# A state-space layer and experts: one scaled piece per unit moves from VectorE to GpSimd, and some buffers shift by six words

## The chip, the cores and the metric

The kernel runs on one NeuronCore of a Trainium2 chip. The metric is the device time of one execution in microseconds (us), lower is better. All arithmetic is float32. Five engines with queues of their own take part: TensorE (PE; its weight loads are shown as PEld), VectorE (DVE), ScalarE (ACT), GpSimd (POOL) and SyncE (SP, which only issues DMAs). They meet at semaphores.

## The reference, cut to what matters

2048 tokens are embedded (C = 192), normalised, and go through a selective state-space layer in both directions, then through eight experts of which each token takes two. What the change touches is the scan:

```python
xz = layernorm(x) @ W_in                       # 192 -> 2 * 384
u  = silu(depthwise_conv1d(xi, conv_w, conv_b))
for each direction d in (forward, backward):
    dt = softplus(u @ Wx[:, :12] @ dt_w + dt_b)          # per token and channel
    B, C = the next 16 and the last 16 columns of u @ Wx # per token and state
    h  = exp(dt * A) * h + (dt * u) * B                  # along the tokens, 16 states per channel
    y  = sum over states of h * C,  + u * D
y  = layernorm(merge of both) * silu(z);  out = y @ W_out + residual
then: layernorm, router (top 2 of 8), h = relu(x @ W1[e] + b1)**2, y = h @ W2[e] + b2
```

## The kernel before, in words

The tokens stand in NG = 4 groups of 512 (GT), a group in TG = 4 tiles of 128, the 384 channels in DB = 3 blocks of 128. A **unit** u is a pair of states in one direction of one group: UG = 16 units a group, NU = 64 in all; `unit_of(u)` gives group, pair and direction. An **item** i = 3u + blk is one block of channels of a unit, a tile of 128 x 1024 (two states by 512 tokens); there are 192.

The stage of the scan (about 184 to 668 us of the span) is a pipeline over four engines, each with its loop written out by hand:

- ACT, for each unit: `exps(u)`, six activations, two per block (L1206), that make the decay exp(dt * A); then `scale_x(u + 1)`, seven activations (L1192), that scale seven of the eight pieces (two states by four tiles, each 128 x 384) of the transposed dt * u by a column of B. A piece lands in `xt(u % 2, n, t)`. `exps(u)` waits for the scans of unit u - 2 (decay is double by direction), `scale_x(u + 1)` for the transposes of unit u - 1 (`s_x_ps`).
- DVE, for each item: `scan(i)` (L818) with the decay from SBUF and the input from PSUM; it waits for the decay, for the transposed input (`s_x_ps`) and for the sum of item i - 4 (`s_sum`; there are four state buffers). Among the scans stand: `scale_rest(u + 2)` (L837), the eighth piece, after the third scan of each unit; `keep_dtu_t` (L844), a copy from PSUM in eight of the 16 units of the first three groups; and, at the start of a group, `keep_y` (L823) and `moments_y` (L635, L638) of the group before.
- POOL, for each item: state = state * C in place (L559), C coming broadcast by DMA (L456) in `c_bc[u % 3]`. In units 4 and 9 of the first three groups it also makes dt * u for the next group, `times_u` (L548).
- PE, for each item: `x_transposes_of(i)`, eight transposes of scaled pieces into a pair of PSUM banks (waits for scan i - 2, and for a new unit for `s_xt_a` and `s_xt_v`); then `add(i - 3)`, eight transposes that add the states into the y banks (waits for `s_mul`). All transposes stand at L1376.

PE's wait for the input of a new unit:

```python
if blk == 0:
    pe.wait_ge(s_xt_a, u + 1)
    pe.wait_ge(s_xt_v, u + 1)
```

After the last item everything waits for `s_sum` = 192: ACT and SP then issue the loads of gates and expert weights (L1236, L477), and the out product, router and experts follow.

Before the stage, DVE and POOL work on softplus: DVE `correction` (L772, L773) and `dt_sum` (L779), POOL L543, and DVE `times_u` for group 0 (L787). In the front part POOL makes the gate terms (L538).

**Where the buffers lie.** They are cut one after another from one SBUF tensor, `arena`, in words of four bytes. All sizes up to `xt_flat` are multiples of 16 words, so `u_all`, `dt_all`, `bt`, `c_bc[1]`, `c_bc[2]`, `decay` and `state` start on a grid of 16 words. Each of the two `xt_flat` has three words more (`DB * (ODD - P)`: the eighth piece has its blocks 129 words apart), so what is cut after them, `dtu_t[1]`, `dtu` and `c_bc[0]`, starts six words off that grid. Hence of the three C buffers, the one of the units with u % 3 = 0 is six words off already before the change, the other two are on the grid. `state`, which is multiplied with them, is on the grid.

Of the kernel before, what the change touches and what calls it, by code (L numbers as in the profile page):

```python
# [8 lines left out]
ALU = mybir.AluOpType  # L9
# [12 lines left out]
DB = DI // P  # L22
NS = 16
RANK = 12
GT = 512
NG = TOK // GT
TG = GT // P
SG = GT // SEQ
PAIR = 2
UG = 2 * (NS // PAIR)  # L30
NU = NG * UG
# [16 lines left out]
BATCHES = (0, 2, 8, 16, 24, 32, SLOTS)  # L48
HH = H // 2
GATE_W = 2 * TG * DI  # L50


class Steps:
# [17 lines left out]
def build(nc, tok, emb, spos, pos, chan, w_in, gb_in, xproj, dt_w, gb_out, w_out, merge, w_route, emb_t,  # L71
          energy, fatigue, gates12, b1, b2, wf1, ws1, hf1, wf2, ws2, hf2, gates_dram, b_rows, x_rows, y_rows, out):
    ctx = ExitStack()
    with ctx:
# [3 lines left out]
        def sem(name):  # L78
            return ctx.enter_context(nc.semaphore(name))
# [57 lines left out]
        used = [0]  # L137

        def cut(shape, dt=FP32, parts=P):
            n = 1  # L140
            for s in shape:
                n *= s
            words = n if dt != BF16 else n // 2
            assert used[0] + words <= ARENA, used[0]
            v = arena[0:parts, used[0]:used[0] + words]
            used[0] += words
            if dt != FP32:
                v = v.bitcast(dt)
            if len(shape) == 2:
                v = v.rearrange("p (a b) -> p a b", b=shape[1])  # L150
            if len(shape) == 3:
                v = v.rearrange("p (a b c) -> p a b c", b=shape[1], c=shape[2])
            if len(shape) == 4:
                v = v.rearrange("p (a b c d) -> p a b c d", b=shape[1], c=shape[2], d=shape[3])
            return v


        u_all = [cut([DB, GT]) for _ in range(NG)]
        y_all = [m.rearrange("p a b -> p (a b)").rearrange("p (t d) -> p t d", d=DI) for m in u_all]
        temps = used[0]  # L160
        dt_all = [[cut([DB, GT]) for _ in range(2)] for _ in range(NG)]
        bt = cut([TILES, 2 * NS])
        fronts = used[0]

        c_bc = [None] + [cut([PAIR, GT]) for _ in range(C_BUFS - 1)]
        decay = [[cut([PAIR, GT]) for _ in range(DB)] for _ in range(2)]
        state = [cut([PAIR, GT]) for _ in range(STATES)]
        ODD = P + 1
        xt_flat = [cut([PAIR * TG * DI + DB * (ODD - P)]) for _ in range(2)]
        dtu_t = [[ln_flat[:, TG * DI * d:TG * DI * (d + 1)].rearrange("p (t c) -> p t c", t=TG) for d in range(2)],  # L170
                 [cut([TG, DI]) for _ in range(2)]]
        def xt(i, n, t, blk=None):

            at, step = DI * (TG * n + t), ODD if (n, t) == (PAIR - 1, TG - 1) else P
            if blk is not None:
                return xt_flat[i][:, at + step * blk:at + step * blk + P]
            return xt_flat[i][:, at:at + DB * step].rearrange("p (b c) -> p b c", b=DB)[:, :, 0:P]
# [141 lines left out]
        s_bt = sem("b_t_ready")  # L319
        s_dtu = sem("dtu_product_ready")  # L320
        s_dtu_ps = sem("dtu_transposed")
        s_dtu_t = sem("dtu_t_ready")
# [20 lines left out]
        s_rstd_y = sem("y_norm_rstd_ready")  # L343
        s_ln_y = sem("y_norm_variance_ready")
        s_xt_a = sem("x_t_scaled_by_scalar")
        s_xt_v = sem("x_t_scaled_by_vector")
        s_x_ps = sem("x_in_banks")
        s_edge = sem("decay_edges_zeroed")
        s_decay = sem("decay_ready")
# [61 lines left out]
        def unit_of(u):  # L411
            g, r = divmod(u, UG)
            return g, r // 2, r % 2
# [76 lines left out]
        def _(pool):  # L490
            g_ = nc.gpsimd
# [53 lines left out]
            def times_u(g, d):  # L545

                pool.wait_ge(s_dtu_ps, TG * (2 * g + d))
                g_.tensor_tensor(dtu, dt_all[g][d], u_all[g], ALU.mult).then_inc(s_dtu, 1)  # L548

            for i in range(ITEMS):  # L550
                u, blk = divmod(i, DB)
                g, r = divmod(u, UG)
                if blk == 0 and r in (4, 9) and g + 1 < NG:
                    times_u(g + 1, r // 9)
                if blk == 0:
                    pool.wait_ge(s_c_ld[u % C_BUFS], 16 * (u // C_BUFS + 1))

                pool.wait_ge(s_scan, i + 1)
                g_.tensor_tensor(state[i % STATES], state[i % STATES], c_bc[u % C_BUFS], ALU.mult).then_inc(s_mul, 1)  # L559


            def add_weights(e, first, second, added):
# [60 lines left out]
        def _(dve):  # L623
            v = nc.vector
# [179 lines left out]
            def scan(i):  # L804

                u, blk = divmod(i, DB)
                d = u % 2
                dve.wait_ge(s_decay, i + 1)
                dve.wait_ge(s_x_ps, i + 1)
                if i >= STATES:  # L810

                    dve.wait_ge(s_sum, i - STATES + 1)
                a = decay[d][blk].rearrange("p n t -> p (n t)")
                x = ps[:, X_BANK + PAIR * (i % 2):X_BANK + PAIR * (i % 2 + 1), :].rearrange("p n t -> p (n t)")
                o = state[i % STATES].rearrange("p n t -> p (n t)")
                if d:
                    a, x, o = a[:, ::-1], x[:, ::-1], o[:, ::-1]
                v.tensor_tensor_scan(o, a, x, 0.0, ALU.mult, ALU.add).then_inc(s_scan, 1)  # L818

            def keep_y(g):  # L820

                dve.wait_ge(s_sum, IG * (g + 1))
                v.tensor_copy(y_all[g].rearrange("p t c -> p (t c)"), y_ps).then_inc(s_yv, 1)  # L823

            def moments_y(g):
                dve.wait_ge(s_yv, g + 1)
                moments(lambda t: y_all[g][:, t, :], TG * g, TG, mv, s_ln_y)

            def scale_rest(u):

                g, pair, d = unit_of(u)
                n = NS * d + PAIR * pair + PAIR - 1
                dve.wait_ge(s_dtu_t, 8 * g + TG * (d + 1))
                if u >= 2:

                    dve.wait_ge(s_x_ps, DB * (u - 1))
                v.tensor_scalar(xt(u % 2, PAIR - 1, TG - 1), dtu_t[g % 2][d][:, TG - 1, :].rearrange("p (b c) -> p b c", b=DB),  # L837
                                bt[:, TG * g + TG - 1, n:n + 1], None, ALU.mult).then_inc(s_xt_v, 1)

            def keep_dtu_t(g, d, t):  # L840

                n = 8 * g + TG * d + t
                dve.wait_ge(s_dtu_ps, n + 1)
                v.tensor_copy(dtu_t[g % 2][d][:, t, :], ps[:, T_BANK, 0:DI]).then_inc(s_dtu_t, 1)  # L844

            dve.wait_ge(s_dtu_t, 2 * TG)
            dve.wait_ge(s_bt, NG)
            scale_rest(0)
            scale_rest(1)
            for g in range(NG):  # L850
                for r in range(UG):
                    for blk in range(DB):
                        scan(IG * g + DB * r + blk)
                        if blk == 1 and g + 1 < NG and 6 <= r < 6 + 2 * TG:
                            keep_dtu_t(g + 1, *divmod(r - 6, TG))
                        if blk == DB - 1 and UG * g + r + 2 < NU:
                            scale_rest(UG * g + r + 2)
                        if g and r == 0 and blk == 1:
                            keep_y(g - 1)
                        if g and r == 0 and blk == 2:  # L860
                            moments_y(g - 1)
# [509 lines left out]
        def _(pe):  # L1371
# [3 lines left out]
            def transpose(o, src, parts, start=True, at=0):  # L1375
                return mm(o, src, ident[at:at + parts, at:at + parts], start=start, stop=True, is_transpose=True, skip_group_check=True)  # L1376
# [13 lines left out]
            for g in range(NG):  # L1390
# [11 lines left out]
                for t in range(TG):  # L1402
                    n = TG * g + t
# [58 lines left out]
            def x_transposes_of(i):  # L1462

                u, blk = divmod(i, DB)
                if blk == 0:
                    pe.wait_ge(s_xt_a, u + 1)
                    pe.wait_ge(s_xt_v, u + 1)
                if i >= 2:

                    pe.wait_ge(s_scan, i - 1)  # L1470
                for n in range(PAIR):
                    for t in range(TG):
                        last = transpose(ps[:, X_BANK + PAIR * (i % 2) + n, P * t:P * t + P], xt(u % 2, n, t, blk), P)
                last.then_inc(s_x_ps, 1)
# [31 lines left out]
            for i in range(ITEMS + LAG):  # L1506
                if i < ITEMS:
                    x_transposes_of(i)
                if i >= LAG:
                    add(i - LAG)  # L1510
                if i < ITEMS and i % DB == DB - 1:
                    g, r = divmod(i // DB, UG)
                    if 2 <= r < 2 + TG:
                        skip_term(g, r - 2)
                    if g + 1 < NG and 5 <= r < 5 + 2 * TG:
                        d, t = divmod(r - 5, TG)
                        pe.wait_ge(s_dtu, 2 * (g + 1) + d + 1)
                        pe.wait_ge(s_dtu_t, 8 * (g + 1) + r - 5)
                        dtu_transposes(g + 1, d, t, T_BANK * GT)
# [200 lines left out]
```

## Time and profile before

| what | us |
|---|---|
| median of 3 runs (lowest, highest) | 1049.5 (1047.43, 1049.77) |
| the profiled execution: its own time | 1040.84 |
| its span, first to last instruction | 1039.1 |

Busy time over the span: PE 764.9 us (74%), DVE 737.8 (71%), ACT 708.7 (68%), POOL 649.2 (62%); mean granted TensorE clock 0.894. Of the 40 slices of the page, the seventh to the twenty-fifth are the stage of the scan. A row of a view by lines reads: line, engine, operation, what it writes <- what it reads, shapes, count | busy us, mean ns of one | idle time of the engine before it and what ended it. A row of a timeline reads: start, us (merged instructions run on), engine, line, operation, names, count, and in brackets the idle time before and its releaser. Durations of neighbours overlap a little on one engine, so the distance from start to start is less than the duration.

### The profile page before, as it was taken

The page shows a single profiled execution, that of the slowest core. Times are in us where ns is not written, and L with a number is a line of the kernel's source. Part 1 is how long each engine was busy: PE and PEld are TensorE (multiplying, and loading weights), DVE is VectorE, ACT ScalarE, POOL GpSimd, SP SyncE. Part 2 cuts the span into 40 slices and gives each one's busy share as a digit, 9 for nine tenths or more (in the row PEclk, how much of TensorE's full clock was granted, in tenths as well). Part 3 has the DMA queues.
Part 4 walks back from the last instruction along what each step waited for, and adds up shares of the span by engine and source line. Part 5 has one row for each costly group of instructions (what it writes and reads, how often), then busy time and mean ns, then how long its engine had stood idle before and what let it go on. Part 6 is the DMA issues. An engine that isn't in the chain of part 4 may idle for free. (4 is left out here: it accounts for less than half of the span.)

```text
span 1039.1 us, 14980 instructions
## 1 busy us (share of the span) xinstructions
PE 764.9 (74%) x5308; PEld 665.1 (64%) x5309; DVE 737.8 (71%) x836; ACT 708.7 (68%) x1189; POOL 649.2 (62%) x359
## 2 busy tenths in 40 slices
PE   0559772787878778789887888656626887999991
PEld 0225321677777777678776877556525877999991
DVE  4898387899999999999999999964155111222224
ACT  0134895999999999899998999324242444565652
POOL 7435555699998999799998999602113656221120
PEclk9969665899999999999999999986655899899996
DMA  4012101112123112212111222299986752000005
GB/s 85 0 61 121 66 26 28 55 61 82 62 81 123 61 65 79 82 62 76 68 62 70 73 82 81 78 314 211 258 188 149 144 129 60 24 19 23 19 23 190
DMA packets 31902, 91.92 MB, mean 88 GB/s; under 512 B 7560, under 2 KB 15264, under 8 KB 30824
## 3 DMA queue, kind: packets, MB, share of 16 engines
q1 hardware_dynamic: 20792, 57.53, 16.4%
q0 software_dynamic: 8352, 27.07, 12.1%
q10 hardware_dynamic: 2704, 6.61, 1.9%
q8 instruction: 32, 0.52, 0.2%
q14 instruction: 22, 0.18, 0.1%
HBM read 77.67 MB, written 13.53 MB: 88 GB/s over the span
## 5 line engine op out<-in xcount | busy, mean ns | idle before, releaser
L1376 PE MATMUL ps<-ident,arena 128*128 128x128 f32 (+1 forms) x3390 | 433.3, 282 | 171.6 <-DVE arena L818 54.7
L1376 PEld LDWEIGHTS ps<-ident,arena 128*128 128x128 f32 (+1 forms) x3390 | 381.0, 144 | 218.4 <-DVE arena L818 70.2
L559 POOL TENSOR_TENSOR arena<-arena 128x1024 f32<-128x1024 f32 x192 | 426.7, 2248 | 44.0 <-DVE arena L818 41.6
L818 DVE TENSOR_TENSOR_SCAN arena<-arena,ps 128x1024 f32<-128x1024 f32 x192 | 428.0, 2271 | 5.0 <-PE ps L1376 3.6
L1206 ACT ACTIVATE arena<-arena,neg_a 128x510 f32<-128x510 f32 x384 | 241.4, 714 | 0.0
L1192 ACT ACTIVATE arena<-arena 128x384 f32<-128x384 f32 x224 | 116.8, 607 | 9.0 <-PE ps L1376 8.9
L1192 ACT ACTIVATE arena<-ln_in,arena 128x384 f32<-128x384 f32 x224 | 116.8, 609 | 5.5 <-PE ps L1376 5.4
L1035 DVE TENSOR_SCALAR ln_in<-ps 128x768 f32<-128x768 f32 x39 | 37.3, 957 | 112.4 <-PE ps L1619 82.0
L618 POOL DMA_INDIRECT y_rows<-arena x39 | 37.9, 971 | 115.1 <-DVE arena L1040 107.6
L1629 PE MATMUL ps<-arena,ln_in 128*128 x468 | 85.4, 332 | 9.8 <-issue 7.2
L1629 PEld LDWEIGHTS ps<-arena,ln_in 128*128 128x128 f32 x468 | 76.9, 194 | 10.5 <-issue 10.4
L1619 PE MATMUL ps<-arena,ln_in 96*128 96x128 f32 x456 | 59.2, 290 | 6.6 <-issue 6.6
L1619 PEld LDWEIGHTS ps<-arena,ln_in 96*128 96x128 f32 x456 | 58.2, 205 | 8.6 <-issue 8.6
L1327 ACT ACTIVATE arena<-ps 96x256 f32<-96x256 f32 x39 | 14.7, 378 | 71.0 <-PE ps L1376 47.7
L1619 PE MATMUL ps<-arena 96*128 96x128 f32 x480 | 59.0, 280 | 1.9 <-issue 1.3
L1619 PEld LDWEIGHTS ps<-arena 96*128 96x128 f32 x480 | 58.0, 196 | 2.6 <-issue 2.5
L1040 DVE COPY arena<-ps 128x192 f32 (+1 forms) x39 | 13.9, 357 | 60.5 <-PE ps L1629 44.6
L543 POOL TENSOR_TENSOR arena<-arena 128x1536 f32<-128x1536 f32 x8 | 37.6, 4698 | 29.1 <-DVE arena L773 29.1
L582 POOL DMA_INDIRECT arena<-x_rows,arena x39 | 37.4, 959 | 27.2 <-issue 16.5
L563 POOL DMA_DIRECT2D arena<-wf x8 | 7.5, 943 | 71.0 <-ACT arena L1273 68.7
L1339 ACT ACTIVATE ln_in<-ln_in 128x768 f32<-128x768 f32 x39 | 32.8, 842 | 20.4 <-DVE ln_in L1035 19.2
L538 POOL TENSOR_TENSOR arena<-arena 128x1536 f32<-128x1536 f32 x8 | 27.3, 3432 | 22.0 <-ACT arena L1126 22.0
(206 smaller groups left out, 830.0 us busy)
## 6 DMA issues: line engine op xcount, KB each, us to landing
arena<-b_rows SPq DMA_DIRECT2D x64, 512.0 KB, 3.5
arena<-ws SPq DMA_DIRECT2D x16, 576.0 KB, 9.3
arena<-wf POOLq DMA_DIRECT2D x16, 576.0 KB
arena<-hf POOLq DMA_DIRECT2D x16, 576.0 KB
gates_dram<-arena SPq DMA_DIRECT2D x4, 1536.0 KB, 5.1
arena<-gates_dram ACTq DMA_DIRECT2D x3, 1536.0 KB, 12.9
arena<-y_rows SPq DMA_DIRECT2D x4, 768.0 KB, 7.2
arena<-gates_dram SPq DMA_DIRECT2D x1, 1536.0 KB, 8.8
```

The costliest lines, as they stand in the source:

```text
L543: g_.tensor_tensor(sp_pos[n % SP], sp_pos[n % SP], sp_w[n % SP], ALU.subtract).then_inc(s_rc, 1)
L559: g_.tensor_tensor(state[i % STATES], state[i % STATES], c_bc[u % C_BUFS], ALU.mult).then_inc(s_mul, 1)
L582: g_.indirect_dma_start(out=slot_rows[:, s, :], out_offset=None, in_=x_rows, in_offset=bass.IndirectOffsetOnAxis(ap=src_row[:, s:s + 1].bi ...
L618: g_.indirect_dma_start(out=y_rows, out_offset=bass.IndirectOffsetOnAxis(ap=dst_row[:, s:s + 1].bitcast(U32), axis=0), in_=slot_rows[:, s, ...
L818: v.tensor_tensor_scan(o, a, x, 0.0, ALU.mult, ALU.add).then_inc(s_scan, 1)
L1035: v.tensor_scalar(h_t[half].rearrange("p (a b) c -> p a (b c)", a=2), ps[:, bank:bank + 2, 0:HH], 0.0, None, ALU.max).then_inc(s_hr, 1)
L1192: last = a.activation(xt(u % 2, n, t), dtu_t[g % 2][d][:, t, :].rearrange("p (b c) -> p b c", b=DB), ACT.Copy, scale=bt[:, TG * g + t, col ...
L1206: last = a.activation(out_a[:, n, :, lo:hi], src[:, :, lo:hi], ACT.Exp, scale=neg_a[:, blk, d, PAIR * pair + n:PAIR * pair + n + 1])
L1339: a.activation(h_t[half], h_t[half], ACT.Square).then_inc(s_h, 1)
L1376: return mm(o, src, ident[at:at + parts, at:at + parts], start=start, stop=True, is_transpose=True, skip_group_check=True)
L1619: last = mm(ps[:, H_BANKS[half] + j // 3, P * (j % 3):P * (j % 3) + P], w1_cur[half][0:KC + k, k, P * j:P * j + P], slot_x_t[half][0:KC + ...
L1629: last = mm(ps[:, 3, 0:C], h_t[half][:, j, :], w2_all[:, bass.ds(e * (HB * C) + j * C, C)], start=j == 0, stop=j == HB - 1)
```

## The change

The eighth piece of each unit is scaled by POOL in place of DVE, with the same shapes. On POOL it stands behind the multiplication of the unit's third item; on DVE it stood behind the scan of the third item. Its semaphore has a new name, and PE waits for that. `dt_all` (and what reuses its place: conv, sz, gate_in, gate_back[0], all cut from `temps`) and `c_bc[1]`, `c_bc[2]` start six words off the grid; after each group of them ten more words bring the next buffer back to it.

```diff
+SKEW, LINE = 6, 16
         u_all = [cut([DB, GT]) for _ in range(NG)]
+        used[0] += SKEW
         temps = used[0]
         dt_all = [[cut([DB, GT]) for _ in range(2)] for _ in range(NG)]
+        used[0] += LINE - SKEW
         bt = cut([TILES, 2 * NS])
         fronts = used[0]
+        used[0] += SKEW
         c_bc = [None] + [cut([PAIR, GT]) for _ in range(C_BUFS - 1)]
+        used[0] += LINE - SKEW
         decay = [[cut([PAIR, GT]) for _ in range(DB)] for _ in range(2)]
...
 # GpSimd
+            def scale_rest(u):
+                g, pair, d = unit_of(u)
+                n = NS * d + PAIR * pair + PAIR - 1
+                pool.wait_ge(s_dtu_t, 8 * g + TG * (d + 1))
+                if u >= 2:
+                    pool.wait_ge(s_x_ps, DB * (u - 1))
+                g_.tensor_scalar(xt(u % 2, PAIR - 1, TG - 1), dtu_t[g % 2][d][:, TG - 1, :].rearrange("p (b c) -> p b c", b=DB),
+                                bt[:, TG * g + TG - 1, n:n + 1], None, ALU.mult).then_inc(s_xt_p, 1)
+            pool.wait_ge(s_bt, NG)
+            scale_rest(0)
+            scale_rest(1)
             for i in range(ITEMS):
...
                 g_.tensor_tensor(state[i % STATES], state[i % STATES], c_bc[u % C_BUFS], ALU.mult).then_inc(s_mul, 1)
+                if blk == DB - 1 and u + 2 < NU:
+                    scale_rest(u + 2)
...
 # VectorE
-            dve.wait_ge(s_bt, NG)
-            scale_rest(0)
-            scale_rest(1)
...
                         scan(IG * g + DB * r + blk)
...
-                        if blk == DB - 1 and UG * g + r + 2 < NU:
-                            scale_rest(UG * g + r + 2)
...
 # TensorE
-                    pe.wait_ge(s_xt_v, u + 1)
+                    pe.wait_ge(s_xt_p, u + 1)
```

## Rows read from the trace of the kernel before

**Rows 1.** Busy time by windows: the scan's stage, and one unit of the last group.

```profile
core 0: us, PE busy (x) PEld busy (x) DVE busy (x) ACT busy (x) POOL busy (x), PEclk, DMA share, GB/s
184.00:668.00 484.00, 394.69 (x3239) 356.62 (x3240) 478.32 (x312) 460.35 (x828) 446.94 (x198) 0.99 0.20 70
...
579.10:586.20 7.10, 6.37 (x57) 5.92 (x56) 7.10 (x5) 7.07 (x15) 6.15 (x4) 1.00 0.26 85
```

**Rows 2.** Lines by form in the scan's stage, 184 to 668 us: VectorE, GpSimd.

```profile
L818 DVE TENSOR_TENSOR_SCAN arena<-arena,ps 128x1024 f32<-128x1024 f32 x192 | 428.0, 2271 | 5.0 <-PE ps L1376 3.6 <-issue 1.1
L837 DVE TENSOR_SCALAR arena<-arena 128x384 f32<-128x384 f32 x32 | 18.9, 591 | 0.0
L844 DVE COPY arena<-ps 128x384 f32<-128x384 f32 x16 | 8.6, 535 | 0.0
...
L559 POOL TENSOR_TENSOR arena<-arena 128x1024 f32<-128x1024 f32 x192 | 426.7, 2248 | 44.0 <-DVE arena L818 41.6 <-issue 0.3
L548 POOL TENSOR_TENSOR arena<-arena 128x1536 f32<-128x1536 f32 x6 | 20.8, 3464 | 0.0
```

**Rows 3.** Timeline, 574 to 597 us, units 51 to 53: VectorE, then ScalarE.

```profile
574.28 6.63 DVE L818 TENSOR_TENSOR_SCAN arena<-arena,ps 128x1024 f32<-128x1024 f32 x3
580.83 0.59 DVE L837 TENSOR_SCALAR arena<-arena 128x384 f32<-128x384 f32 x1
581.34 6.63 DVE L818 TENSOR_TENSOR_SCAN arena<-arena,ps 128x1024 f32<-128x1024 f32 x3
...
582.96 3.77 ACT L1206 ACTIVATE arena<-arena,neg_a 128x510 f32<-128x510 f32 x6
586.63 3.64 ACT L1192 ACTIVATE arena<-arena 128x384 f32<-128x384 f32 x7
590.17 3.77 ACT L1206 ACTIVATE arena<-arena,neg_a 128x510 f32<-128x510 f32 x6
```

**Rows 4.** Who ScalarE waited for in the stage: us in total, times, longest.

```profile
ACT arena L1192 <- PE ps L1376: 14.3, 10, 3.9
```

**Rows 5.** Timeline around the start of the second group, 303 to 328 us.

```profile
305.47 4.46 DVE L818 TENSOR_TENSOR_SCAN arena<-arena,ps 128x1024 f32<-128x1024 f32 x2
309.84 1.74 DVE L823 COPY arena<-ps 128x1536 f32<-128x1536 f32 x1
316.45 6.61 DVE L818 TENSOR_TENSOR_SCAN arena<-arena,ps 128x1024 f32<-128x1024 f32 x3
318.75 9.02 PE L1376 MATMUL ps<-ident,arena 128*128 128x128 f32 x64 [2.97 <-DVE arena L818]
319.95 3.66 ACT L1192 ACTIVATE arena<-arena 128x384 f32<-128x384 f32 x7 [2.10 <-PE ps L1376]
```

**Rows 6.** Timeline of GpSimd, 298 to 345 us: items 47, 48 and 49, 56, 57 to 59.

```profile
305.13 2.00 POOL L559 TENSOR_TENSOR arena<-arena 128x1024 f32<-128x1024 f32 x1 [0.18 <-DVE arena L818]
307.89 4.70 POOL L559 TENSOR_TENSOR arena<-arena 128x1024 f32<-128x1024 f32 x2 [0.76 <-DVE arena L818]
...
330.19 2.00 POOL L559 TENSOR_TENSOR arena<-arena 128x1024 f32<-128x1024 f32 x1 [0.18 <-DVE arena L818]
332.95 7.05 POOL L559 TENSOR_TENSOR arena<-arena 128x1024 f32<-128x1024 f32 x3 [0.76 <-DVE arena L818]
```

**Rows 7.** One line each, all its instructions: durations in ns, min/median/max, first and last start.

```profile
L1192 ACT ACTIVATE arena<-arena x224: 597/602/632, 296.1 to 654.6; 128x384 f32<-128x384 f32 x112
L1192 ACT ACTIVATE arena<-ln_in,arena x217: 596/609/628, 187.9 to 534.2; 128x384 f32<-128x384 f32 x109
...
L818 DVE TENSOR_TENSOR_SCAN arena<-arena,ps x192: 2252/2267/2289, 186.4 to 662.8; 128x1024 f32<-128x1024 f32 x192
```

**Rows 8.** Lines by form of GpSimd before the stage, 0 to 184 us.

```profile
L520 POOL TENSOR_TENSOR ln_in<-ln_in,arena 128x512 f32<-128x512 f32 x2 | 3.2, 1592 | 0.2
...
L500 POOL TENSOR_SCALAR_AFFINE_SELECT ident<-ident 128x128 f32<-128x128 f32 x1 | 1.4, 1386 | 0.2 <-POOL ident L498 0.2
L508 POOL TENSOR_SCALAR_AFFINE_SELECT before<-before 128x128 f32<-128x128 f32 x1 | 0.3, 292 | 0.1
```

**Rows 9.** Timeline, 145 to 190 us: softplus, and the start of the stage.

```profile
147.01 4.88 POOL L543 TENSOR_TENSOR arena<-arena 128x1536 f32<-128x1536 f32 x1 [2.69 <-DVE arena L773]
148.63 4.88 DVE L787 TENSOR_TENSOR arena<-arena 128x1536 f32<-128x1536 f32 x1
...
171.39 4.87 POOL L543 TENSOR_TENSOR arena<-arena 128x1536 f32<-128x1536 f32 x1 [2.69 <-DVE arena L773]
176.35 1.76 DVE L779 TENSOR_TENSOR arena<-arena 128x1536 f32<-128x1536 f32 x1 [3.38 <-POOL arena L543]
178.03 1.75 DVE L787 TENSOR_TENSOR arena<-arena 128x1536 f32<-128x1536 f32 x1
184.20 3.78 ACT L1206 ACTIVATE arena<-arena,neg_a 128x510 f32<-128x510 f32 x6
186.36 4.47 DVE L818 TENSOR_TENSOR_SCAN arena<-arena,ps 128x1024 f32<-128x1024 f32 x2 [0.80 <-PE ps L1376]
```

**Rows 10.** Timelines of the end of the stage, 640 to 690 us.

```profile
651.88 13.16 DVE L818 TENSOR_TENSOR_SCAN arena<-arena,ps 128x1024 f32<-128x1024 f32 x6
654.30 12.90 POOL L559 TENSOR_TENSOR arena<-arena 128x1024 f32<-128x1024 f32 x6
655.10 3.79 ACT L1206 ACTIVATE arena<-arena,neg_a 128x510 f32<-128x510 f32 x6
667.25 1.09 PE L1376 MATMUL ps<-ident,arena 128*128 128x128 f32 x8 [0.86 <-POOL arena L559]
668.83 0.92 ACTq L1236 DMA_DIRECT2D arena<-gates_dram  x2
```

More of the change, by code:

```diff
@@ L345, in build @@
         s_xt_a = sem("x_t_scaled_by_scalar")
-        s_xt_v = sem("x_t_scaled_by_vector")
+        s_xt_p = sem("x_t_scaled_by_gpsimd")
         s_x_ps = sem("x_in_banks")
@@ L827, in moments_y @@
                 moments(lambda t: y_all[g][:, t, :], TG * g, TG, mv, s_ln_y)
[L829 to L838, printed above, removed]
             def keep_dtu_t(g, d, t):
```

## The prediction

> **What bounds the kernel now.** I read busy time by windows first, because the change lies in one stage. In the 484 us of the scan's stage DVE is busy 478.3, ACT 460.4, POOL 446.9, PE 394.7 [rows 1]: VectorE looks like the bound, and ScalarE stands right behind it. Whether DVE's 17.9 us of lead or the whole work taken from it is the gain, the mean doesn't tell, so I went to the distances from start to start. Where both engines run without idle time, a unit takes DVE 581.34 - 574.28 = 7.06 us (three scans 6.55, then L837 0.51) and ACT 590.17 - 582.96 = 7.21 us (six exponentials 3.67, that is 0.61 each, and seven scalings 3.54) [rows 3]. So in a plain unit ACT is already the slower of the two. DVE is the slower one only in the 24 units that also hold a copy L844 (0.54 long, some 0.47 from start to start: 7.53 a unit), and at the three starts of a group, where the copy of y and its moments stand between scans. There the scans fall behind ACT, until ACT has to wait for a transposed input; the view of waits adds this up: 14.3 us in 10 waits, the longest 3.9 us, and ScalarE waited for nothing else in the stage [rows 4]. The mechanism stands in the timeline of the second group's start: from scan 48 to scan 51 it takes 316.45 - 305.47 = 10.98 us in place of 7.06; at scan 51's end PE does the transposes that ACT waits for, and ACT resumes at 319.95 after 2.10 us idle [rows 5]. The stage is therefore ScalarE's 460 us and 14.3 us in which it is held up, with a start and a tail.
>
> **What leaves VectorE.** 64 instructions L837 (32 from each source, 591 ns, 37.7 us busy) [rows 2]. From start to start each costs DVE 0.51 us [rows 3], 32.6 us in all. A unit of DVE falls to 6.55 us, with the copy to about 7.02, both under ACT's 7.21. None of these 32.6 us shortens the path beyond the point at which ACT waits no more: the next bound is 0.15 us a unit away in a plain unit.
>
> What is left of ACT's waits? I follow the worst place, the start of a group. In steady state a unit's first scan can start some 1.4 us after ACT's first exponential of that unit (two of 0.61 us, and about 0.15 for the semaphore). From scan 48 to scan 51 it then takes 10.98 - 0.51 = 10.5 us, so scan 51 starts 11.9 us after the first exponential of unit 16, ends at 14.1, and with the transposes (1.2 us, from 318.75 to 319.95 [rows 5]) the input is free at 15.3. ACT asks for it two units and six exponentials later, at 2 x 7.21 + 3.67 = 18.1. It has 2.8 us to spare, where it lacked 2.1. The delay of 3.3 us is worked off at 0.66 us a plain unit, before the copies begin in the seventh unit; in units with a copy it doesn't grow (7.02 against 7.21). I count all 14.3 us as gained; the other end is that half of them stay.
>
> **What comes to GpSimd, and what leaves it.** Its multiplications L559 are of two kinds. Item 47 (unit 15) and item 56 (unit 18) take 2.00 us each, while items 48 and 49 together take 4.70 and items 57 to 59 take 7.05, which is 2.37 each and 2.34 from start to start [rows 6]. Units with u % 3 = 0 use c_bc[0], the one C buffer that is six words off the grid already; the mean of all 192, 2248 ns [rows 2], is what one third at 2.00 and two thirds at 2.37 give. The change puts the other two C buffers on the same offset: 2.00 us for all 192 (1.96 from start to start), 128 x 0.38 = 48.6 us less on POOL. The six L548 (3.46 us) read dt off and u on the grid from now on: 1536 columns at the same saving per column would be 2.9 us; at worst they stay at 3.46. The other engines' work on the shifted buffers I cost at nothing: ACT's scalings from dtu_t[1], six words off already, take 602 ns, those from ln_in 609 [rows 7], and that difference, either way, is the bound.
>
> The added instruction isn't in the trace of POOL: one input, 128 x 384, a scalar per partition. From below it is bounded by the one-input operation on 128 x 128, 0.29 us on its second run; from above by L520, 1.59 us for 512 columns of two inputs in pieces of 64, or 3.1 ns a column: 1.19 us [rows 8]. At L559's 1.95 ns a column it would be 0.75; one input should cost less than two, and I take 0.6. A unit of POOL is then 3 x 1.96 + 0.6 = 6.5 us (6.2 to 7.1), under ACT's 7.21, and the stage 64 x 6.5 + 6 x 2.9 = 433 us, or 471 with the upper ends, against 460 of ACT. Behind the new instruction on POOL is queued the next unit's first multiplication; it waits for a scan that ends 2.2 us or more after the one before, so 1.96 + 0.6 leaves it at most 0.4 us late, and that is caught up by the next two. Who waits for the new instruction is PE, with the transposes of unit u + 2's first item and all that follows in its queue. It comes there only after scan 3u + 4, 4.4 us after scan 3u + 2, while POOL is ready 0.15 + 1.96 + 0.6 = 2.7 us after it: hidden by 1.7 us. That cover is gone when L548 (2.9 us) stands in front, six times: then the transposes come some 1.2 us later, of which the scan sees 0.3 to 0.8. It is late with respect to an ACT that has slack of several us by the count above, so the cost is nothing.
>
> A rule that speaks against this sum is in the Trainium skill, "Perfetto Trace Analysis", section "Optimizing Scalar/DVE Operations": VectorE and GpSimd share a read port, so moving work between the two may not help. It is the third rival below. The price by the skill's "GPSIMD Engine Reference", section "3.1 Elementwise — side-by-side cycle accounting" (about 1.8 cycles of 1.2 GHz for an element at best), would be an estimated 0.58 us before its dispatch; with it the sum stays as it is, and no row here shows that rate.
>
> **The start.** POOL ends its last L543 at 176.26 and goes on with scale_rest(0), whose inputs are there. DVE starts the two-input L779 at 176.35 [rows 9], and with that L787, PE's transposes and ACT's first exponential (184.20). Two such operations hinder each other: DVE's L787, 1.75 us by itself, took 4.88 beside POOL's L543 [rows 9]. So L779 waits for scale_rest(0) to finish: 0.4 us late, and up to 1.7 if the first of its kind takes 1.1 us longer, as the first of the one-input operations did (1.39 against 0.29) [rows 8]. I take 0.4; below, nothing. Scan 0 no longer waits for two L837, but ACT's pace takes that back.
>
> **The sum.** ACT's first exponential of the last unit is at 655.10 [rows 10]: 14.3 less for its waits, 0.4 more for the start. DVE's six last scans start at 651.88 and end at 665.04, so scan 189 starts at 658.4, 3.3 us behind that exponential; with DVE in step it is 1.4: 1.9 less. The last multiplication (ends at 667.20) is in step in both. So `s_sum` is full 14.3 + 1.9 - 0.4 = 15.8 us earlier, and the loads at 668.83 with all that follows them move as one: that stretch works on the same data with the same instructions. Edits at nothing: L538 in the front part (0.5 us shorter each, ACT doesn't wait for POOL there), the shifted gate and C transfers. The profiled execution took 1040.84 (span 1039.1): 1025.0 after. The timed runs lie 8.7 above it, at 1049.5, and the stage is the same program there, so the same difference is taken off: 1033.7.
>
> **Rivals.** (a) Half of ACT's waits stay, because POOL's late pieces and the groups' starts fall together: -8 us, 1041.5. For it: DVE's margin in units with a copy is only 0.2 us. Against it: 2.8 us of slack in the worst place.
> (b) GpSimd becomes the bound. The stage of 480.8 us (186.36 [rows 9] to 667.20 [rows 10]) holds 192 x 1.96 + 6 x 2.9 = 393.7 us of its old work, so from (480.8 - 393.7) / 64 = 1.36 us per new instruction the kernel is slower than before. If the change between two kinds of operation cost each time what the first one did, 0.6 + 1.1 = 1.7 us, the stage would be 502.5, +21.7: 1071. For it: only the 1.39 us. Against it: the second one-input operation ran in 0.29 us though others of different kinds stood between them.
> (c) The shared port: each new instruction holds up a scan for its length, 64 x 0.6 = 38 us, and DVE is at 7.1 a unit again: no change, 1049.5. Against it: the 192 scans lie between 2252 and 2289 ns, whether POOL is busy beside them or idle [rows 7]; their second input comes from PSUM.
> (d) The offset does nothing for c_bc[1] and [2]: POOL has 128 x 2.34 + 64 x 1.96 + 6 x 3.46 + 64 x 0.6 = 484 us of work in a stage of 480.8: about +3, 1052. Against it: [rows 6].
>
> **How the numbers follow.** Forecast 0.72 (1030 to 1038 by the unknown start, the last bits of lag and the runs' own spread of 2.3 us), (a) 0.15, (b) 0.05, (c) 0.04, (d) 0.04. What a measurement of this kernel can tell from no change is 0.2%, 2.1 us. Faster: forecast, (a), less 0.01 for (a) at its weakest: 0.86; the same: (c), part of (d): 0.07; slower: (b), the rest of (d): 0.07. The range 1029 to 1043 takes in nearly all of (a) and leaves out (b) to (d), 0.13, and 0.03 at the edges.
>
> **What would show it.** L559 at 2.00 us for all three C buffers; the new POOL operation 0.3 to 1.2 us; no wait of ACT for PE in the stage; a unit 7.21 us long on ACT with idle time on DVE before the scans, 0.2 to 0.7 us a unit; the loads of L1236 at 653. I am wrong if ACT still waits, if POOL runs without gaps, if scans get longer than 2.27 us, or if ACT's first exponential comes later than 186.

## The result, and the profile after

The median is 1043.4 us (20 runs, 1039.2 to 1048.3) against 1047.9 for before (20 runs, 1044.2 to 1049.9): ratio 0.996, interval 0.9948 to 0.9971, so 3.0 to 5.4 us faster. The forecast gain was 15.8 us. Busy time by windows over the same stretch as in [rows 1]:

```profile
core 0: us, PE busy (x) PEld busy (x) DVE busy (x) ACT busy (x) POOL busy (x), PEclk, DMA share, GB/s
184.00:668.00 484.00, 408.75 (x3240) 364.32 (x3240) 451.97 (x252) 459.33 (x827) 472.01 (x261) 0.97 0.21 71
```

VectorE has lost 26 us: its 64 instructions left, and some work from behind the stage, which now ends earlier, moved into the window. GpSimd is the busiest engine now, 472.0 us where it had 446.9. Its lines by form, 184 to 680 us (columns as in [rows 2]):

```profile
L578 POOL TENSOR_TENSOR arena<-arena 128x1024 f32<-128x1024 f32 x192 | 383.4, 2062 | 9.0 <-DVE arena L840 8.3
L563 POOL TENSOR_SCALAR arena<-arena 128x384 f32<-128x384 f32 x32 | 42.2, 1317 | 0.0
L563 POOL TENSOR_SCALAR arena<-ln_in,arena 128x384 f32<-128x384 f32 x31 | 40.1, 1293 | 7.2 <-ACT ln_in L1186 7.2
L553 POOL TENSOR_TENSOR arena<-arena 128x1536 f32<-128x1536 f32 x6 | 17.7, 2946 | 0.0
```

The multiplications fell, from 2248 ns in the mean to 2062 (2.00 us was forecast), and `times_u` (L553 now) from 3464 to 2946, as forecast. The new instruction takes 1.3 us, more than twice the 0.6 of the prediction and over the upper end of its bounds, 1.19. In a second profile of the same kernel (a0 below) the multiplications took 2012 ns and the new instruction 1.26 us, so this profile is somewhat slow in both. A part of the timeline of the last group, GpSimd then VectorE, then ScalarE, answers to [rows 3]:

```profile
609.27 1.34 POOL L563 TENSOR_SCALAR arena<-arena 128x384 f32<-128x384 f32 x1
610.48 6.01 POOL L578 TENSOR_TENSOR arena<-arena 128x1024 f32<-128x1024 f32 x3
616.38 1.33 POOL L563 TENSOR_SCALAR arena<-arena 128x384 f32<-128x384 f32 x1
...
607.56 6.64 DVE L840 TENSOR_TENSOR_SCAN arena<-arena,ps 128x1024 f32<-128x1024 f32 x3 [0.46 <-PE ps L1382]
614.68 6.64 DVE L840 TENSOR_TENSOR_SCAN arena<-arena,ps 128x1024 f32<-128x1024 f32 x3 [0.48 <-PE ps L1382]
...
608.74 3.76 ACT L1212 ACTIVATE arena<-arena,neg_a 128x510 f32<-128x510 f32 x6
615.95 3.76 ACT L1212 ACTIVATE arena<-arena,neg_a 128x510 f32<-128x510 f32 x6
```

GpSimd runs without a gap, 616.38 - 609.27 = 7.11 us a unit (1.21 for the new instruction from start to start, 5.90 for three products), and VectorE idles 0.5 us a unit behind it, waiting for PE, which waits for GpSimd. 7.11 is still below ScalarE's 7.21, so plain units alone would cost nothing. It costs at `times_u`: with a reserve of 0.1 us a unit, GpSimd would need 29 units to work off another 2.9 us, and `times_u` stands 5 or 11 units apart. Timeline of GpSimd, then VectorE, then PE around unit 9, where VectorE starts unit 10:

```profile
254.85 1.32 POOL L563 TENSOR_SCALAR arena<-ln_in,arena 128x384 f32<-128x384 f32 x1
256.06 2.98 POOL L553 TENSOR_TENSOR arena<-arena 128x1536 f32<-128x1536 f32 x1
258.93 5.99 POOL L578 TENSOR_TENSOR arena<-arena 128x1024 f32<-128x1024 f32 x3
...
255.78 2.28 DVE L840 TENSOR_TENSOR_SCAN arena<-arena,ps 128x1024 f32<-128x1024 f32 x1
261.71 4.59 DVE L840 TENSOR_TENSOR_SCAN arena<-arena,ps 128x1024 f32<-128x1024 f32 x2 [3.66 <-PE ps L1382]
...
259.09 7.45 PE L1382 MATMUL ps<-ident,arena 128*128 128x128 f32 x51 [3.01 <-POOL arena L553]
```

GpSimd was some 3 us behind the scans before it took up `times_u` (a lag is counted from the end of an item's scan to the start of its multiplication). Behind it the lag is 5.8 us, PE stands idle for 3.01 us and VectorE for 3.66. PE's wait here is not for the new instruction and not for a late product, but for `times_u` itself. At the end of the sixth and the tenth unit of a group PE turns to the first transposes of the next group's dt * u in one direction, and they stand in its queue before the next unit's input:

```python
pe.wait_ge(s_dtu, 2 * (g + 1) + d + 1)
...
dtu_transposes(g + 1, d, t, T_BANK * GT)
```

PE's waits for `times_u` in the stage, before and after:

```profile
PE ps L1376 <- POOL arena L548: 3.2, 3, 1.2
```

```profile
PE ps L1382 <- POOL arena L553: 8.2, 3, 3.0
```

These are the three in the tenth units. Behind the three `times_u` in the fifth units the late products alone hold PE and with it VectorE, up to 4.4 us at once. The waits of the stage, VectorE's and ScalarE's (7.0 of the second row lie before the very first scan; the last row answers to [rows 4]), show what came of it:

```profile
DVE arena L840 <- PE ps L1382: 22.8, 25, 4.4
DVE arena L840 <- ACT arena L1212: 8.3, 4, 7.0
...
ACT arena L1198 <- PE ps L1382: 12.3, 6, 3.0
```

ScalarE's waits, all of which were to go, fell only from 14.3 to 12.3 us. Three of the six (6.3 us) come behind `times_u`, at 349, 388 and 472 us. The other three (6.0 us) still stand at the starts of groups, as in this row of ScalarE's timeline, which answers to the last of [rows 5]:

```profile
319.32 2.13 ACT L1198 ACTIVATE arena<-arena 128x384 f32<-128x384 f32 x4 [1.84 <-PE ps L1382]
```

From the first scan to the end of the last multiplication the stage took 478.6 us (before: 480.8); in two other profiles of kernels that run like before (e0 and e5 below) 482.6 and 480.7, in a second one of this kernel (a0) 478.2. The means differ by 3.0 us, the lower end of the measured gain; what the runs show above that is within their interval. The profiled execution of this kernel is nevertheless 3.4 us longer than before's, 1044.23 against 1040.84. From the last multiplication to the first matrix product of the experts (797.05 before, 797.10 now) it took 132.1 us in place of 129.9, and from there to the last product of the experts 224.5 in place of 221.0, with the same instructions at a lower granted clock. Windows of the experts, before and after, one row each:

```profile
802.00:1018.50 216.50, 197.15 (x1456) 193.13 (x1454) 50.91 (x78) 111.04 (x151) 74.92 (x79) 0.96 0.23 54
```

```profile
802.00:1022.00 220.00, 201.78 (x1459) 198.24 (x1458) 51.08 (x78) 111.21 (x151) 74.86 (x79) 0.93 0.23 53
```

The eleven profiles of the table below have 129.3 to 132.1 us for the first of these stretches, in no order that follows the change, so the prediction's "all that follows them move as one" holds only to some 3 us. The experts vary too, and between chips by more (before took 1047.9, 1023.1, 1048.8 and 1021.3 us in the four measurements of this study); I therefore compare by ratios to before on the same chip, and by the length of the stage.

### The profile page after: what moved, and what is told of

Read it like the earlier page. It is cut to its first block, busy times and chain, and to the rows that moved or that the text cites. A ratio compares the mean times of both kernels' runs of the same rounds, so it can differ in the third digit from the quotient of the medians.

```text
span 1042.5 us, 14980 instructions
## 1 busy us (share of the span) xinstructions
PE 782.7 (75%) x5308; PEld 676.9 (65%) x5309; DVE 705.0 (68%) x772; ACT 708.2 (68%) x1189; POOL 670.9 (64%) x423
## 3 DMA queue, kind: packets, MB, share of 16 engines
q1 hardware_dynamic: 20792, 57.53, 16.4%
## 4 chain that ended last, share of the span: by engine, by line
PE 22%; POOL 16%; DMA 8%; issue 6%; DVE 3%; ACT 2%; another core or an unknown queue 1%; ACTq 0%; DVEq 0%; POOLq 0%; SPq 0%
POOL arena L578 13%; PE ps L1625 11%; PE ps L1635 8%; DMA x_rows<-arena 4%; POOL arena L563 3%; PE ps L1382 2%; DMA arena<-gates_dram 1%; DMA arena<-wf 1%; ACT arena L1279 1%; DMA arena<-hf 1%; DVE arena L840 1%; PE ps L1549 1%; POOL arena L553 0%; DMA arena<-x_rows,arena 0%
## 5 line engine op out<-in xcount | busy, mean ns | idle before, releaser
L1382 PE MATMUL ps<-ident,arena 128*128 128x128 f32 (+1 forms) x3390 | 446.4, 286 | 163.8 <-POOL arena L578 35.4
L1382 PEld LDWEIGHTS ps<-ident,arena 128*128 128x128 f32 (+1 forms) x3390 | 388.6, 146 | 214.8 <-issue 66.7
L578 POOL TENSOR_TENSOR arena<-arena 128x1024 f32<-128x1024 f32 x192 | 383.4, 2062 | 9.0 <-DVE arena L840 8.3
L1625 PE MATMUL ps<-arena 96*128 96x128 f32 x480 | 64.0, 295 | 4.1 <-issue 3.5
L1625 PEld LDWEIGHTS ps<-arena 96*128 96x128 f32 x480 | 63.2, 211 | 4.8 <-issue 4.8
L548 POOL TENSOR_TENSOR arena<-arena 128x1536 f32<-128x1536 f32 x8 | 37.6, 4699 | 30.1 <-DVE arena L795 30.1
L563 POOL TENSOR_SCALAR arena<-ln_in,arena 128x384 f32<-128x384 f32 x32 | 41.3, 1291 | 7.2 <-ACT ln_in L1186 7.2
```

What stands on the lines that cost most here:

```text
L548: g_.tensor_tensor(sp_pos[n % SP], sp_pos[n % SP], sp_w[n % SP], ALU.subtract).then_inc(s_rc, 1)
L563: g_.tensor_scalar(xt(u % 2, PAIR - 1, TG - 1), dtu_t[g % 2][d][:, TG - 1, :].rearrange("p (b c) -> p b c", b=DB), bt[:, TG * g + TG - 1, ...
L1625: last = mm(ps[:, H_BANKS[half] + j // 3, P * (j % 3):P * (j % 3) + P], w1_cur[half][0:KC + k, k, P * j:P * j + P], slot_x_t[half][0:KC + ...
```

## The experiments

Stage below is the time from the first scan to the end of the last multiplication, and waits are ScalarE's for PE in it, both from one profile of each kernel. Three kernels that run like before (before, e0, e5) spread over 1.9 us of stage, so smaller differences than that tell nothing.

| kernel | ratio to before (interval) | stage us | waits us |
|---|---|---|---|
| before | 1 | 480.8 | 14.3 |
| after | 0.9960 (0.9948 to 0.9971) | 478.6 | 12.3 |
| e0, before again | 1.0002 (0.9989 to 1.0016) | 482.6 | 16.4 |
| a0, after again | 0.9958 (0.9938 to 0.9977) | 478.2 | 12.0 |
| e1, offset alone | 0.9928 (0.9908 to 0.9949) | 475.5 | 8.3 |
| e2, move alone | 1.0408 (1.0387 to 1.0428) | 524.5 | 46.3 |
| e3, no eighth piece | 0.9827 (0.9807 to 0.9846) | 463.7 | 0 |
| e4, offset of C alone | 0.9950 (0.9929 to 0.9971) | 476.3 | 10.2 |
| e5, offset of four words | 0.9997 (0.9985 to 1.0008) | 480.7 | 14.3 |
| v1, 18 pieces back on VectorE | 0.9828 (0.9803 to 0.9852) | 464.4 | 0 |
| v2, product form on GpSimd | 0.9804 (0.9785 to 0.9823) | 462.5 | 0 |

**e0, the control, and a0.** Both unchanged.

> The kernel before, unchanged, as its own control, with a second profile. Both theories: ratio 1.000 within 0.3%. If the profiled execution of before (1040.84 us, clock 0.894) was a lucky one in the part behind the scan's stage, this one's part from the full sum on is 373 to 379 us where that one had 370.8, and the stage's end lies within 1 us of 668.3; if it was no luck, the part is 371 again.

> The changed kernel, unchanged, beside the same runs of before as the next ones, since chips differ. All theories: 0.996 of before within 0.3%, so between the kernel with the offset alone (0.993) and before.

Both ratios came out as expected. The last multiplication of e0 ended at 670.2 us, 3.0 later than in before, where the stage was to end within 1 us of it: 1.2 of that stand before the first scan, 1.8 in the stage. The part of e0 behind the stage isn't comparable, for that chip ran the experts faster; whether before's first profile was a lucky one stays open.

**e1 and e2, the two halves of the change.** In e1 the offset stands in before; e2 is after with it set to zero:

```diff
-SKEW, LINE = 6, 16
+SKEW, LINE = 0, 0
```

> Before, with the six-word offset alone; the eighth piece stays on VectorE. My theory (VectorE at 7.06 us a plain unit and 7.53 with a copy bounds it, GpSimd's time is slack): L559 falls to 2.0 us for all three C buffers, the stage shortens only by the few us in which VectorE waited for a late sum, 0 to 3 us, 1045 to 1048. Rival (the offset alone brings the whole gain of the change): 4.5 us, 1043.4.

> After, with the offset set to zero: the piece on GpSimd, C buffers on the grid. My theory (GpSimd bounds the changed kernel, with 1.21 us from start to start for the new instruction): two units in three take it 3 x 2.34 + 1.2 = 8.2 us, one 7.1, mean 7.85; 62 units and six times_u of 3.4 us are 507 us against 479 of the stage before: 1072 to 1080, slower than before by 2.5 to 3%. Rival (GpSimd has slack, the loss of the forecast gain lies in ports or clocks): 1043 to 1048.

e2 decides for GpSimd as the bound: with its products at 2.37 us on two buffers in three it costs 4.1%. That is more than I had expected, since my sum left two of the 64 units out: 64 x 7.85 + 6 x 3.4 = 523 us against a stage of 524.5. e1 missed both expectations: the offset alone gains 0.7%, more than the whole change, though I had called GpSimd's time slack. So on top of the offset the move costs some 3 us, by the stage (475.5 against 478.6 and 478.2); the intervals of the ratios just touch. Where e1 gains shows at unit 21, behind a `times_u`, in VectorE's timeline of before and of e1:

```profile
344.64 2.27 DVE L818 TENSOR_TENSOR_SCAN arena<-arena,ps 128x1024 f32<-128x1024 f32 x1
347.86 4.62 DVE L818 TENSOR_TENSOR_SCAN arena<-arena,ps 128x1024 f32<-128x1024 f32 x2 [0.94 <-PE ps L1376]
352.39 0.59 DVE L837 TENSOR_SCALAR arena<-arena 128x384 f32<-128x384 f32 x1
353.52 2.29 DVE L818 TENSOR_TENSOR_SCAN arena<-arena,ps 128x1024 f32<-128x1024 f32 x1 [0.54 <-issue]
```

```profile
341.58 6.64 DVE L823 TENSOR_TENSOR_SCAN arena<-arena,ps 128x1024 f32<-128x1024 f32 x3
348.13 0.60 DVE L842 TENSOR_SCALAR arena<-arena 128x384 f32<-128x384 f32 x1
348.63 4.46 DVE L823 TENSOR_TENSOR_SCAN arena<-arena,ps 128x1024 f32<-128x1024 f32 x2
```

In before that unit takes 8.88 us (344.64 to 353.52), in e1 7.05: GpSimd, 3.5 us behind, held up a sum, and with faster products it doesn't. In e1 VectorE has no idle time at all between the first scan and the last (its only wait in the stage, 1.7 us, is for the first scan), so there VectorE alone sets the length.

**e3, the upper limit.** From unit 2 on no engine scales the eighth piece:

```diff
-                if blk == DB - 1 and u + 2 < NU:
-                    scale_rest(u + 2)
...
-                    pe.wait_ge(s_xt_p, u + 1)
+                    pe.wait_ge(s_xt_p, min(u + 1, 2))
```

> After, but from unit 2 on nobody scales the eighth piece (that part of the computation is left out; the old contents of the piece are used). My theory (with GpSimd out of the way ScalarE bounds, 7.21 us a unit, without waits): GpSimd 5.9 us a unit with idle time, ScalarE's waits for PE 0 to 2 us, the sum is full at 652 to 654 us where it was 668, and the time is 14 to 17 us under before: 1031 to 1034. Rival (something else than GpSimd's new instruction holds the stage, as PE's order or VectorE's copies at the groups' starts): it stays at 1040 to 1043.

As my theory had it, and a little more: 1.7% is 18 us of before's 1047.9, where 14 to 17 were expected. VectorE's timeline in the last group:

```profile
583.55 6.64 DVE L838 TENSOR_TENSOR_SCAN arena<-arena,ps 128x1024 f32<-128x1024 f32 x3 [0.59 <-ACT arena L1210]
590.79 6.64 DVE L838 TENSOR_TENSOR_SCAN arena<-arena,ps 128x1024 f32<-128x1024 f32 x3 [0.59 <-ACT arena L1210]
```

A unit is ScalarE's 7.24 us, VectorE waits 0.59 for its exponentials, and ScalarE waits for nothing. That is the stage that the prediction described; the last multiplication ended at 650.2 where its sum gave 651.4.

**p1, the price of the operation.** After, with GpSimd operations behind its last wait, each started only when the one before is done, and each twice (`one` is a scalar per partition in SBUF; `O` and `A0` are the places of the output and of the first input in one buffer, both on a grid of 16 words). It ran once, in 1093.3 us; only the durations of its operations are used:

```diff
+                st.then(g_.tensor_scalar(blocks(O, ODD), blocks(A0), one, None, ALU.mult))
+                st.then(g_.tensor_scalar(flat[:, O:O + DI], flat[:, A0:A0 + DI], one, None, ALU.mult))
+                st.then(g_.tensor_scalar(flat[:, O:O + DI], flat[:, A0:A0 + DI], 0.5, None, ALU.mult))
...
+                for off in (0, 2, 4, 6, 8, 12, 14):
+                    st.then(g_.tensor_tensor(flat[:, O:O + 1024], flat[:, A0:A0 + 1024], flat[:, 2048 + off:3072 + off], ALU.mult))
```

> After, with a row of GpSimd operations put behind its last wait, each twice and each waiting for the one before; their results are used nowhere, and VectorE's last sums wait for their end. It prices the new instruction. If the price of 1.3 us lies in the three pieces with a step of 129 words, the flat 128 x 384 takes 0.5 to 0.7 us; if in the scalar read from SBUF, the form with a constant does; if it is a fixed price of the operation, 128 columns take 1.0 us or more and 1024 columns 2.0; if it is the rate, 128 columns take 0.5 and 1024 3.2. A product with a broadcast column (two inputs) takes 0.8 to 1.1. The product of 1024 columns takes 2.37 at offsets of 0 and 16 words and 2.0 at 6; at which of 2, 4, 8, 12 and 14 it is fast is open: a step of 16 words between hindering addresses says fast at all of them, a step of 8 says slow at 8, of 4 slow at 4, 8 and 12.

By lines and forms: L652 is the kernel's own form, L653 flat, L654 with a constant, L655 and L656 with 128 and 1024 columns; L657 and L658 are products with a broadcast column, flat and in three pieces:

```profile
L656 POOL TENSOR_SCALAR arena<-arena,mv 128x1024 f32<-128x1024 f32 x2 | 5.7, 2844 | 0.2
L652 POOL TENSOR_SCALAR arena<-arena,mv 128x384 f32<-128x384 f32 x2 | 2.5, 1249 | 1.6 <-DMA y_rows<-arena 1.5
L653 POOL TENSOR_SCALAR arena<-arena,mv 128x384 f32<-128x384 f32 x2 | 2.5, 1244 | 0.2
L654 POOL TENSOR_SCALAR arena<-arena 128x384 f32<-128x384 f32 x2 | 2.3, 1170 | 0.2
...
L657 POOL TENSOR_TENSOR arena<-arena 128x384 f32<-128x384 f32 x2 | 1.7, 828 | 0.2
L658 POOL TENSOR_TENSOR arena<-arena 128x384 f32<-128x384 f32 x2 | 1.7, 827 | 0.2
L655 POOL TENSOR_SCALAR arena<-arena,mv 128x128 f32<-128x128 f32 x2 | 1.2, 604 | 0.2
```

The price is the rate: (2844 - 604) / 896 = 2.5 ns a column and 0.28 us fixed. The three pieces make no difference, a constant in place of the scalar from SBUF only 0.08 us. L653 stands behind an operation of its own kind and costs the same as L652, so a change of kind costs nothing here. The same result as a product of two tensors takes 0.83 us. The timeline gives the seven offsets, here 0, 2, 4 and 6; 8 and 12 took 2.34 as 4 did, 14 took 2.00:

```profile
1033.29 2.35 POOL L660 TENSOR_TENSOR arena<-arena 128x1024 f32<-128x1024 f32 x1
1035.71 2.00 POOL L660 TENSOR_TENSOR arena<-arena 128x1024 f32<-128x1024 f32 x1
1037.79 2.34 POOL L660 TENSOR_TENSOR arena<-arena 128x1024 f32<-128x1024 f32 x1
1040.21 2.00 POOL L660 TENSOR_TENSOR arena<-arena 128x1024 f32<-128x1024 f32 x1
```

**v1, pieces kept off GpSimd around `times_u`.**

```diff
+        def on_vector(u):
+            g, r = divmod(u, UG)
+            return g + 1 < NG and r in (3, 4, 5, 8, 9, 10)
...
```

> After, but the pieces made in units 3, 4, 5, 8, 9 and 10 of the first three groups (around the two times_u) go to VectorE, 18 of 64; the other 46 stay on GpSimd. My theory (GpSimd at 7.1 us a unit keeps up with ScalarE's 7.21, but the 2.9 us of each times_u, which it can't work off, hold PE at the new unit's piece): the stalls of 3 to 5 us at those units go, ScalarE's waits fall from 12 to 0 to 3 us, time 12 to 17 us under before, near the kernel without any eighth piece (0.983). Rival (it is the price of every new instruction that counts, or VectorE's fill with copies): 4 to 8 us under before.

Slightly better than I expected (18 us where 12 to 17 stood): 46 pieces at the full price of 1.25 us are harmless once the six `times_u` have room. It was GpSimd's sum, not each instruction, that cost. v1 takes 18 x 1.21 = 22 us off that sum and clears the surroundings of `times_u` at the same time; whether 18 pieces taken away elsewhere would have done as well wasn't tried.

**v2, the same piece at a lower price.** All 64 pieces stay on GpSimd:

```diff
-                g_.tensor_scalar(xt(u % 2, PAIR - 1, TG - 1), dtu_t[g % 2][d][:, TG - 1, :].rearrange("p (b c) -> p b c", b=DB),
-                                bt[:, TG * g + TG - 1, n:n + 1], None, ALU.mult).then_inc(s_xt_p, 1)
+                g_.tensor_tensor(xt(u % 2, PAIR - 1, TG - 1), dtu_t[g % 2][d][:, TG - 1, :].rearrange("p (b c) -> p b c", b=DB),
+                                bt[:, TG * g + TG - 1, n:n + 1].unsqueeze(2).to_broadcast([P, DB, P]), ALU.mult).then_inc(s_xt_p, 1)
```

> After, with the piece on GpSimd made as a product of two tensors (B's column broadcast over the 384 columns) in place of a product with a scalar: same inputs, same output, all 64 pieces on GpSimd. My theory (only the price of 1.25 us was wrong in the prediction; at the probe's 0.83 us GpSimd takes 6.7 us a unit and the prediction's sum holds): no waits of ScalarE, the stage 463 to 466 us from the first scan to the last multiplication (after: 478), 14 to 18 us under before, ratio 0.982 to 0.987. Rival (whatever stands on GpSimd there hinders PE's order, only leaving units out helps): ratio 0.990 to 0.996.

It gains 2.0%, a little more than expected, and beats both kernels. Its GpSimd timeline:

```profile
585.99 0.86 POOL L563 TENSOR_TENSOR arena<-arena 128x384 f32<-128x384 f32 x1
586.77 5.97 POOL L578 TENSOR_TENSOR arena<-arena 128x1024 f32<-128x1024 f32 x3
592.65 0.87 POOL L563 TENSOR_TENSOR arena<-arena 128x384 f32<-128x384 f32 x1
```

6.66 us a unit, 0.78 of it for the piece. One edit of the price alone brings the gain that was forecast, and more: 2.0% of 1047.9 is 20 us, where 15.8 were forecast. The stage accounts for 18.3 us of it; the rest lies within the spread of what stands before and behind the stage.

**e4 and e5, which offset matters.** e4 is e1 without the two lines around `dt_all`; e5 sets `SKEW = 4` in e1.

> Before, with the offset for the two C buffers only, dt stays on the grid. My theory (the offset's gain of 7 us comes from multiplications that no longer fall behind after times_u, 0.35 us each, and times_u's own 0.5 us adds little): 5 to 7 us under before. Rival (times_u's 0.5 us each, through the offset of dt, carries the gain): 0 to 2 us under before.

> Before, with an offset of four words in place of six for c_bc[1], c_bc[2] and dt. The probe was slow at 0, 4, 8 and 12 words and fast at 2, 6 and 14. My theory (only the place within a line of four words counts): L559 2.37 us for two C buffers in three, 2.0 for c_bc[0], which keeps its six words, and the time within 0.3% of before. Rival (any offset from the states' grid of 16 words helps): 2.0 us for all, 5 to 7 us under before.

e4 gains 0.5% and shortens the stage by 4.5 us, as my theory had it: most of the offset's gain is that of the C buffers. What dt adds (0.8 us of the stage) isn't resolved. e5 gains nothing, as expected, and L564 keeps its 2.37 us on two buffers of three.

## Why the prediction was wrong

- **"ACT is already the slower of the two"; all its waits go, -14.3, and the tail, -1.9.** Right as a limit: e3, v1 and v2 have stages of 462.5 to 464.4 us without such waits.
- **"One input should cost less than two, and I take 0.6."** This step failed. The instruction measured 1.25 (alone and in v1) to 1.3 us, 1.21 from start to start, and made GpSimd the engine that sets the length of the stage. The neighbour that drew the estimate down, 0.29 us for 128 columns in one input, is of another operation; the one at issue takes 0.60 for 128. The sum with the measured price is 64 x 7.09 + 6 x 2.87 = 471 us of GpSimd. Measured are 470.8 us busy in the stage (472.0 less the piece made at 184.06), 2.4 until the first scan was done and 5.4 of other idle time, most of it at the groups' starts: 478.6, which is the stage. The prediction had worked out 471 for the upper ends (its terms give 470 to 475, by which ends are taken; that it equals the measured sum is chance), saw it above ScalarE's 460, and didn't give that case a chance of its own. It also left out that GpSimd stands idle at times.
- **"That cover is gone when L548 stands in front ... so the cost is nothing."** Wrong for the same reason: the count assumed a GpSimd in step with the scans. At 7.11 us a unit it stands up to 3.4 us behind, and at `times_u` 4 to 6, so that VectorE loses 3.7 us in one place and 4.4 in another, where 0.3 to 0.8 were allowed. PE's own wait for `times_u`, 3.2 us in three waits already in before and 8.2 now, was not in the count at all.
- **"It has 2.8 us to spare" at the start of a group.** That fell with the same step: from scan 48 to scan 51 it took 11.85 us (303.10 to 314.95) where 10.5 were reckoned, with VectorE waiting for PE and PE for GpSimd, and ScalarE still lost 1.84 us. Without GpSimd's lag (e3, v1, v2) it loses nothing there, so the count itself was sound.
- **Rival (a), half of ScalarE's waits stay: 1041.5.** It came nearest, with late pieces and groups' starts as its cause, and a chance of 0.15. It was still too mild: 12.3 of 14.3 us stayed.
- **Rival (b), GpSimd as the bound, slower from 1.36 us an instruction.** The right mechanism, with a break-even set too high: it took GpSimd as never idle. At 1.21 the stage is only 3.0 us shorter than before's, or 0.05 for each of the 62 instructions in it, so my estimate from the measured stages is a break-even near 1.26. The kernel ended up just below it. Its alternative price, 1.7 us for a change of kind at each instruction, isn't there: among products, the instruction takes 1.21 from start to start.
- **The offset.** c_bc[0] was the right witness for the other two. But its gain was missed as one of its own: GpSimd's lags cost before some 5 to 6 us of the stage already (e1), which the prediction booked under VectorE.
- **The start.** L801 (L779 before) took 2.07 us beside the new instruction in place of 1.76 in [rows 9]: 0.3 late, 0.4 forecast. The number was near by luck: L801 didn't wait for the new instruction to end but ran beside it, and waiting would have cost some 1.1 us at a price of 1.25. The port's rival (c) fell: the 192 scans lie between 2253 and 2289 ns, as in [rows 7].

## What to carry to other kernels

Before work is moved to an engine, give that engine's whole sum with the upper price of the new operation, its bursts included, and if it passes the next bound, make it a case of its own. An operation that the trace doesn't show has no price from a neighbour of another kind, even with fewer inputs; try another form of the same result when it proves dear. An engine without reserve per period turns each rare burst into a stall of everyone behind it.

## What the runs showed of the hardware

On GpSimd a product with a scalar costs 2.5 ns a column plus 0.28 us (p1). A product of two tensors costs (1999 - 864) / 640 = 1.8 ns plus 0.18 us there (1999 ns for 1024 columns, 864 for 384, at offset 6): two inputs are faster than one in these two operations. The product of two tensors runs at 2.00 us for 1024 columns when the inputs' starts are 2, 6 or 14 words apart, and at 2.34 when 0, 4, 8 or 12. Among these, multiples of four words, 16 bytes, are slow and the others fast. Odd distances weren't tried, and one input stood on the grid of 16 words in every case, so whether the distance counts or the place of the other input is not told apart.

The Trainium skill, "GPSIMD Engine Reference", section "3.1 Elementwise — side-by-side cycle accounting", gives about 2.6 cycles an element as the floor of `tensor_tensor`, an estimated 2.2 ns at its 1.2 GHz. The slow case here comes near it, (2340 - 992) / 640 = 2.1 ns, and the fast case, 1.8 ns, lies below that floor. Its section "4.1 Engine selection" calls one-input work on GpSimd roughly line-rate. The 2.5 ns above don't agree: VectorE made the same piece in 0.59 us [rows 2], GpSimd in 1.25.
